# Mamba scan: five of 32 products with B move to ScalarE with time on the partitions, and GpSimd's share is dealt anew

## The reference, cut to what matters

```python
x_in = rn @ in_w.T                         # rn: normalised tokens, 4 x 1024 x 256
x = silu(causal_conv(x_in))                # E = 512 channels
delta = softplus(x @ wd1.T @ wd2.T + wd2_b)
A = -exp(A_log)                            # 512 x 16
Bm, Cm = x @ wB.T, x @ wC.T                # N = 16 values per token each
def step(h, inp):                          # over time
    h = exp(d_l[:, :, None] * A) * h + (d_l * x_l)[:, :, None] * b_l[:, None, :]
    y_l = einsum('ben,bn->be', h, c_l)
```

## Time and profile before

| | us |
|---|---|
| median of 3 runs | 1860.4 (1860.34 to 1862.27) |
| the profiled execution, own time | 1861.13 |
| its span, first to last instruction | 1859.4 |
| VectorE busy over the span | 1471.9 (79%) |
| GpSimd busy | 1100.7 (59%) |
| ScalarE busy | 1074.5 (58%) |
| TensorE matmuls busy | 1708.3 (92%) |

### The profile page before, as it was taken

How to read it: one execution, slowest core, us unless ns; L and a number is a source line. 1 busy time by engine, 2 the same in 40 slices (tenths; PEclk the granted TensorE clock), 3 DMA queues, 4 the chain that set the end, 5 groups by cost and what they waited for, 6 DMA issues and landing times. The chain is left out here.

```text
span 1859.4 us, 26380 instructions
## 1 busy us (share of the span) xinstructions
PE 1708.3 (92%) x9245; PEld 1343.9 (72%) x9245; DVE 1471.9 (79%) x2310; ACT 1074.5 (58%) x1871; POOL 1100.7 (59%) x711
## 2 busy tenths in 40 slices
PE   6888989899898989966889999999999899999999
PEld 2455566565666666655778888888888788888888
DVE  4889999999999999999787767776345586666664
ACT  5877787778778787777534444443443444444442
POOL 2889999999999999999842222220454332222220
PEclk9898999999999999978999999999999999999999
DMA  6223333233333233244011111121000011111111
GB/s 200 81 79 99 107 93 102 87 112 90 108 93 102 94 104 100 95 148 144 7 35 35 35 35 35 35 57 24 7 0 0 1 46 43 46 38 46 46 46 46
DMA packets 113918, 125.63 MB, mean 68 GB/s; under 512 B 18816, under 2 KB 66048, under 8 KB 113664
## 3 DMA queue, kind: packets, MB, share of 16 engines
q1 hardware_dynamic: 113792, 124.03, 22.9%
HBM read 95.14 MB, written 4.72 MB: 54 GB/s over the span
## 5 line engine op out<-in xcount | busy, mean ns | idle before, releaser
L383 POOL TENSOR_TENSOR m_U<-m_U,m_C 128x1024 f32<-128x1024 f32 x255 | 600.6, 2367 | 26.2 <-DVE m_U L890 15.9
L525 PEld LDWEIGHTS m_y<-ident,m_U 128*128 128x128 f32 x2048 | 252.0, 148 | 117.0 <-issue 71.3
L890 DVE TENSOR_TENSOR_SCAN m_U<-m_dA,m_carry,m_U 128x512 f32<-128x512 f32 x256 | 310.8, 1265 | 5.0 <-ACT m_dA L758 4.6
L525 PE MATMUL m_y<-ident,m_U 128*128 128x128 f32 x2048 | 284.4, 285 | 29.2 <-POOL m_U L383 29.0
L890 DVE TENSOR_TENSOR_SCAN m_U<-m_dA,m_U 128x512 f32<-128x512 f32 x256 | 296.2, 1206 | 11.5 <-ACT m_dA L758 8.2
L758 ACT ACTIVATE m_dA<-high,m_negA 128x512 f32<-128x512 f32 x256 | 172.4, 685 | 74.1 <-DVE m_U L890 73.8
L758 ACT ACTIVATE m_dA<-even,m_negA 128x512 f32<-128x512 f32 x256 | 170.8, 684 | 56.1 <-DVE m_U L890 55.1
L1165 POOL TENSOR_TENSOR SW<-g_Rt 128x512 f32<-128x512 f32 x32 | 40.8, 1306 | 253.5 <-DMA g_CT<-SW 235.2
L1165 POOL TENSOR_TENSOR SW<-f_Rt 128x512 f32<-128x512 f32 x32 | 42.0, 1340 | 229.2 <-DMA f_CT<-SW 225.5
L506 PE MATMUL m_psB<-m_stack,m_pick 128*128 128x512 f32 x196 | 101.3, 517 | 33.5 <-DVE m_U L873 33.2
L873 DVE TENSOR_TENSOR m_U<-even,m_psB 128x1024 f32<-128x1024 f32 x100 | 120.0, 1200 | 12.4 <-PE m_psB L506 12.1
(11 more groups left out here) (389 smaller groups left out, 4416.4 us busy)
## 6 DMA issues: line engine op xcount, KB each, us to landing
m_C<-bc_rows SPq DMA_DIRECT2D x256, 256.0 KB, 3.2
m_B<-bc_rows SPq DMA_DIRECT2D x60, 256.0 KB, 3.6
f_CT<-SW SPq DMA_DIRECT2D x128, 64.0 KB, 2.1
g_CT<-SW SPq DMA_DIRECT2D x128, 64.0 KB, 2.0
even<-in_ffn_w SPq DMA_DIRECT2D x16, 256.0 KB, 4.8
f_z_raw<-f_turned_z SPq DMA_DIRECT2D x112, 32.0 KB, 1.9
g_z_raw<-g_turned_z SPq DMA_DIRECT2D x112, 32.0 KB, 1.9
out<-res SPq DMA_DIRECT2D x7, 512.0 KB, 2.8
```

The source lines that it names most:

```text
L383: pool.tensor_tensor(u, u, C[:, M % C_RING, :].unsqueeze(1).to_broadcast([P, PE_E, CHUNK]), ALU.mult).then_inc(hc_ready, 1)
L525: last = nc.tensor.matmul(y[:, t, j * P:(j + 1) * P], U[:, M % U_RING, j, t * P:(t + 1) * P], ident[:, :], start=False, stop=n == N - 1, i ...
L890: nc.vector.tensor_tensor_scan(u, dA[:, s % A_RING, :], u, carry[:, e, n:n + 1] if q else 0.0, ALU.mult, ALU.add).then_inc(scan_done, 1)
```

## The change

Chunk 0 keeps its products as they were. In chunks 1 to 7, units 12 and 14 of the first pass and 2, 4 and 15 of the second (slots 12, 14, 18, 20, 31) are "turned". ScalarE makes their product two units ahead with time on the partitions: B is then one number for each partition, a scale operand, and the product is four activations of 128x256. TensorE turns the result back, four transposes for each half, into the places of the `dA` ring; the decays of such a unit go to an SBUF tile `dAT` instead. The scan reads its decay from `dAT` and its product from PSUM. New jobs turn dx (`tr0` to `tr3`) and B (`bt`) once a chunk. GpSimd's units become (3, 6, 8, 10) and (6, 8, 10, 13) in odd chunks, (3, 6, 9) and (7, 11) in even ones from chunk 2. To make room in SBUF, `C` has three buffers instead of eight and `B` one instead of two; SP issues the fetch of a B row two units earlier than before. Two late jobs (`high0`, `high1`) move to slots 26 and 28, and `FETCH` moves from 8 to 9 units into the last chunk.

```diff
-    U_RING, C_RING, A_RING, B_RING = 6, 8, 3, 2
-    ON_POOL, AHEAD = ((3, 7, 10, 14), (4, 9, 14), (3, 7, 11, 14), (3, 6, 10, 14)), 3
+    U_RING, C_RING, A_RING = 6, 3, 3
+    ON_POOL, AHEAD, B_AHEAD = [((3, 7, 10, 14), (4, 9, 14))] + [((3, 6, 8, 10), (6, 8, 10, 13)), ((3, 6, 9), (7, 11))] * 4, 3, 2
+    TURNED, TURN_AHEAD = [((), ())] + [((12, 14), (2, 4, 15))] * (CHUNKS - 1), 2
...
-                 11: ("cv3",), 12: ("cv3+",), 13: ("out0",), 14: ("out0+",), 15: ("low",), 16: ("low+",),
+                 11: ("cv3",), 12: ("cv3+", "tr2"), 13: ("out0",), 14: ("out0+",), 15: ("tr3", "low"), 16: ("low+",),
...
-                 27: ("out1",), 28: ("out1+",), 29: ("back0",), 30: ("back1",),
+                 27: ("out1",), 28: ("out1+", "tr0"), 29: ("back0",), 30: ("back1",), 31: ("tr1", "bt"),
...
-                if M in pool_units:
-                    i = BEFORE[M]
-                    need(sp, pool_mult, i - B_RING + 1)
-                    sp.dma_start(B[:, i % B_RING, :],
-                                 bc_rows[q, n:n + 1, :].to_broadcast([P, CHUNK])).then_inc(B_ready[i % B_RING], 16)
+                if M + B_AHEAD in pool_units:
+                    n_b = place(M + B_AHEAD)[3]
+                    assert n_b >= B_AHEAD
+                    need(sp, pool_mult, POOL_BEFORE[M + B_AHEAD])
+                    sp.dma_start(B[:, :], bc_rows[q, n_b:n_b + 1, :].to_broadcast([P, CHUNK])).then_inc(B_ready, 16)
...
+            def turn_product(M, j):
+                s = PE_E * M + j
+                pe.wait_ge(UT_ready, TURNED_BEFORE[M] + 1)
+                pe.wait_ge(scan_done, s - A_RING + 1)
+                for t in range(TILES):
+                    last = nc.tensor.transpose(dA[:, s % A_RING, t * P:(t + 1) * P],
+                                               U[:, M % U_RING, j, t * P:(t + 1) * P], ident[:, :])
+                last.then_inc(UT_turned, 1)
...
             for M in range(ALL_UNITS):
-                if M + 2 < ALL_UNITS and M + 2 not in pool_units:
+                if M + 2 in dve_units:
                     spread_B(M + 2)
+                if M + 1 in turned_units:
+                    turn_product(M + 1, 0)
                 for name, k in parts_of(PE_AT, M):
                     part(name, k)
+                if M + 1 in turned_units:
+                    turn_product(M + 1, 1)
...
-                nc.scalar.activation(dA[:, s % A_RING, :], delta[q][:, e, :], ACT.Exp,
+                to = dAT[:, s % PE_E, :] if s // PE_E in turned_units else dA[:, s % A_RING, :]
+                nc.scalar.activation(to, delta[q][:, e, :], ACT.Exp,
                                      scale=negA[:, e, n:n + 1]).then_inc(dA_ready, 1)
+            def product(M):
+                c, q, p, n = place(M)
+                for e in range(PE_E * p, PE_E * (p + 1)):
+                    wait_freed(act, f"tr{e}", c)
+                wait_freed(act, "bt", c)
+                act.wait_ge(nsum_done, M - U_RING + 1)
+                for t in range(TILES):
+                    last = nc.scalar.activation(U[:, M % U_RING, :, t * P:(t + 1) * P], dxT[:, pair(p), t, :], ACT.Copy,
+                                                scale=BT[:, t, n:n + 1])
+                last.then_inc(UT_ready, 1)
...
                     decay(PE_E * (M + 1))
                     decay(PE_E * (M + 1) + 1)
+                if M + TURN_AHEAD in turned_units:
+                    product(M + TURN_AHEAD)
...
+                decay, product = dA[:, s % A_RING, :], u
+                if M in turned_units:
+                    dve.wait_ge(UT_turned, PE_E * TURNED_BEFORE[M] + j + 1)
+                    decay, product = dAT[:, j, :], dA[:, s % A_RING, :]
...
-                nc.vector.tensor_tensor_scan(u, dA[:, s % A_RING, :], u, carry[:, e, n:n + 1] if q else 0.0,
+                nc.vector.tensor_tensor_scan(u, decay, product, carry[:, e, n:n + 1] if q else 0.0,
```

More of the change, by code:

```diff
@@ L129, in mamba @@
         U = sb("U", [P, U_RING, PE_E, CHUNK])
+        pick32 = U[:, 0, 0, 0:2 * N]
         C = sb("C", [P, C_RING, CHUNK])
-        B = sb("B", [P, B_RING, CHUNK])
+        B = sb("B", [P, CHUNK])
+        dxT = sb("dxT", [P, KE, TILES, P])
+        BT = sb("BT", [P, TILES, N])
+        dAT = sb("dAT", [P, PE_E, CHUNK])
         rows = sb("rows", [2 * N, CHUNK])
@@ L151, in mamba @@
         B_full, rows_ready, rows_out = sem("B_full"), sem("rows_ready"), sem("rows_out")
-        B_ready, pool_mult = [sem(f"B_ready{i}") for i in range(B_RING)], sem("pool_mult")
+        B_ready, pool_mult = sem("B_ready"), sem("pool_mult")
+        UT_ready, UT_turned = sem("UT_ready"), sem("UT_turned")
         C_ready = [sem(f"C_ready{i}") for i in range(C_RING)]
@@ L182, in mamba @@
                            (12, "turn0", 9), (12, "turn1", 9), (14, "query", 9), (16, "square", 10), (18, "sum", 11),
-                           (19, "square", 11), (20, "norm", 10), (21, "high0", 0), (22, "turn0", 10),
+                           (19, "square", 11), (20, "norm", 10), (22, "turn0", 10),
                            (22, "turn1", 10), (23, "norm", 11), (24, "query", 10), (25, "turn0", 11),
-                           (25, "turn1", 11), (26, "high1", 0), (27, "query", 11), (29, "back1", CHUNKS - 1)]}
+                           (25, "turn1", 11), (26, "high0", 0), (27, "query", 11), (28, "high1", 0), (29, "back1", CHUNKS - 1)]}
         FIRST_GATE = 10
@@ L191, in mamba @@
         BEHIND = {"out0": -1, "out0+": -1, "out1": -1, "out1+": -1, "gate1": -1, "back2": -1, "back3": -1,
-                  "gate0": 0, "back0": 0, "back1": 0, "silu_g": 0, "sum": 2, "square": 2, "factors": 2, "norm": 2, "double": 2}
+                  "gate0": 0, "tr2": 0, "tr3": 0, "back0": 0, "back1": 0, "silu_g": 0, "sum": 2, "square": 2, "factors": 2, "norm": 2, "double": 2}
         ASKED = dict(enumerate((4, 1, 5, 0), CHUNKS))
@@ L199, in parts_of @@
             late = [(name, k) for slot, name, k in at["late"] if c == CHUNKS - 1 and slot == i]
-            chunks = [(name, k) for name, k in chunks if 0 <= k < CHUNKS and (name, k) != ("back1", CHUNKS - 1)]
+            chunks = [(name, k) for name, k in chunks if 0 <= k < CHUNKS and (name, k) != ("back1", CHUNKS - 1)
+                      and (k > 0 or name[:2] != "tr")]
             return chunks + late
@@ L239, in place, with before @@
             return c, c % 2, i // N, i % N
-        pool_units = [M for M in range(ALL_UNITS) if M % N in ON_POOL[M // N % (2 * PASSES)]]
-        BEFORE = [len([m for m in pool_units if m < M]) for M in range(ALL_UNITS)]
+        pool_units = [M for M in range(ALL_UNITS) if M % N in ON_POOL[M // UNITS][M // N % PASSES]]
+        turned_units = [M for M in range(ALL_UNITS) if M % N in TURNED[M // UNITS][M // N % PASSES]]
+        dve_units = [M for M in range(ALL_UNITS) if M not in pool_units and M not in turned_units]
+        def before(units):
+            return [len([m for m in units if m < M]) for M in range(ALL_UNITS + 1)]
+        POOL_BEFORE, TURNED_BEFORE, DVE_BEFORE = before(pool_units), before(turned_units), before(dve_units)
         def pair(p):
@@ L247, in mamba @@
         SECOND_LAST = UNITS * (CHUNKS - 1)
-        FETCH, PARTS = SECOND_LAST + C_RING, PIECES * KE
+        FETCH, PARTS = SECOND_LAST + 9, PIECES * KE
         block = ctx.enter_context(nc.Block())
@@ L443, in part @@
                     last = mm(take(name, k), [(rnT[:, d, t:t + P], skw[:, d, :]) for d in range(KD)])
+                elif name[:2] == "tr":
+                    e = int(name[2])
+                    pe.wait_ge(dx_ready, KE * k + e + 1)
+                    out = take(name, k)
+                    for t in range(TILES):
+                        last = nc.tensor.transpose(out[:, t * P:(t + 1) * P], dx[q][:, e, t * P:(t + 1) * P],
+                                                   ident[:, :])
+                elif name == "bt":
+                    pe.wait_ge(rows_ready, k + 1)
+                    out = take(name, k)
+                    for t in range(TILES):
+                        last = nc.tensor.transpose(out[:, t * 2 * N:(t + 1) * 2 * N], rows[:, t * P:(t + 1) * P],
+                                                   ident[0:2 * N, 0:2 * N])
                 elif name[:2] == "cv":
@@ L584, in _ @@
             pe.wait_ge(scan_done, PE_E * ALL_UNITS)
[L585 removed]
+            pe.wait_ge(mult_done, len(dve_units))
             pe.wait_ge(gate_done, PASSES * CHUNKS)
@@ L908, in _ @@
             for M in range(ALL_UNITS):
-                if M + 1 < ALL_UNITS and M + 1 not in pool_units:
+                if M + 1 in dve_units:
                     mult(M + 1)
```

33 lines of the change are left out of this document (20 added, 13 removed), and 6 rows, old and new, of the table ACT_AT.

## The result

The changed kernel takes 1873.05 us, median of 6 runs (1869.8 to 1876.3), beside 1862.6 for the kernel before in the same rounds. The ratio is 1.006, 95% interval 1.0046 to 1.0073: slower, by 0.6%. I had forecast 1847 and a range up to 1871. The six executions form two groups, three of 1869.8 to 1871.3 us and three of 1874.8 to 1876.3, and the profiled one is of the second.

What follows compares the result with a forecast made beforehand. VectorE sets the pace, TensorE and GpSimd close behind. Gains of 3.6 us (chunks 1, 3, 5), 6.3 (2, 4, 6) and 4.6 (7), together 14.5, off 1861.1 gave 1846.6, forecast 1847; 8-in-10 range 1829 to 1871.

Steps and rivals of the forecast that it cites:

- The rings and the C landings: C ring of three: landings of 3.3 us, at most 4.1, hidden in 4.7; as a rival 1858 us, chance 0.06.
- the 4 us that I had bounded: Scans of turned units, decay in SBUF and product in PSUM: no change taken, 0.06 us for 70 scans as either end.
- Behind silu_x: Slots 10 to 15: ScalarE's products and a copy delay silu_x, costing VectorE 2.0 us in each of chunks 1 to 6.
- Behind dt0 in odd chunks: Slot 19 behind the gate: unit 20's transposes delay dt0 by 0.44 us and VectorE arrives 1.13 sooner, +1.55 us.
- My own sign of being wrong: One of the listed signs that the forecast is wrong: VectorE's waits over 7 us in odd chunks.
- GpSimd allows at most 33 us: Seven chunks of GpSimd busy time: 710 us against 743.5 now, so a gain of at most 33 us, as much as VectorE's relief.
- I charged 1.0 us of new wait: Chunk 7: 1.0 us in all, for DMA landings of up to 6.9 us at its start beside the FFN weights.
- I took 0.6 us a chunk of new wait: TensorE's added transposes, 100.5 us busy in an odd chunk: 0.6 us of new wait; ends 0 and 4.4.
- VectorE's relief: 29 fewer products on VectorE at 1.13 us: 32.8 us, 5.65 in an odd chunk and 3.4 in an even one.
- I had let 2.0 us of the waits for psB and GpSimd go: Chunks 2, 4, 6: of the waits ending there, 3.9 us in chunk 2, 2.0 go; 2.1 us gained each.
- The rival "ScalarE decides": ScalarE's product takes 2.35 us, on the path four times a chunk, and unit 20's decay comes later: 1872 us, chance 0.14.
- The clock rival: More transposes and fewer spreads lower TensorE's clock in steady chunks to chunk 7's 0.86: 56 us more, 1917 us, chance 0.05.

Runs made afterwards that it cites:

- Four ahead: The changed kernel, but GpSimd makes its product four units ahead instead of three, shares unchanged: 1868.8 us, 1.0043 to the kernel before.
- unit 29 given away: The changed kernel, but VectorE makes unit 29's product in odd chunks, GpSimd seven instead of eight there: 1869.4 us, 1.0042 to the kernel before.
- fewer activations: The changed kernel with one of the four ScalarE activations of each turned product: 1860.65 us, 0.9991 to the kernel before.
- fewer transposes: The changed kernel with one of the four TensorE transposes that turn back each half of a product: 1872.5 us, 1.0053 to the kernel before.
- another order: The changed kernel, but TensorE turns a product's second half ahead of the slot's jobs, not behind them: 1876.0 us, 1.0081 to the kernel before.
- the spaced version: The two repairs together, plus four turned units (8, 12, 18, 31) instead of five in chunks 1 to 6, GpSimd's units re-dealt: 1860.5 us, 0.9992.
- The two repairs together: The changed kernel with chunk 7 dealt as before and GpSimd four units ahead in all chunks: 1862.7 us, 1.0002 to the kernel before.
- the run that changes chunk 7 alone: The changed kernel, but chunk 7 has the old deal, no turned unit and no turning jobs: 1871.1 us, 1.0056 to the kernel before.

## Why the prediction was wrong

**What held.** The product at 1.69 us (1.7 taken). The transposes: eight in 1.04, the last 0.27 included. The rings and the C landings, 3.2 us and at most 4.4 in chunk 3, cost nothing. The turned scan takes 15 ns longer (1273 for 1258 ns with a carry, 1212 for 1197 without), about 1 us in 70 scans, inside the 4 us that I had bounded. Behind silu_x I had 2.3 us of wait in all (2.0 on top of 0.29): measured 1.54, and 0.62 for the turned half of unit 14 ahead of it, 2.2. Behind dt0 in odd chunks 2.7: measured 1.69, and 0.88 for psB ahead of it, 2.6. That these sums agree is in part luck: I had put all of it down to ScalarE's late decay, and a third of it is TensorE's. My own sign of being wrong, waits of VectorE over 7 us in odd chunks, came with 8.6.

**The step that failed first: GpSimd.** "GpSimd allows at most 33 us" treated it as a sum of busy time, 101.8 in an odd chunk. A sum does not say when a product is there. The product of unit M is issued three units ahead, behind the C product of unit M-3. From the end of the scans of M-3 to the start of those of M VectorE takes 6.9 us where it makes two products of its own between. Less GpSimd's product, 2.4, and the C product of M-3, 2.3, this leaves the C products about 2.2 us to lag behind the scans. That time is the same in both kernels (467.5 to 474.4 for unit 30 before, 466.1 to 473.1 for unit 29 after); what grew is the lag. From unit 22 on, two units cost GpSimd 8.2 us (456.62 to 464.82: two C products, a product and a dx job) and VectorE only 5.9 (451.70 to 457.55), since every second product is GpSimd's. So GpSimd lagged 4.6 us at unit 26, ahead of its product for unit 29. In the kernel before it lagged 1.4 us at unit 27, ahead of its product for unit 30. This cost 3.6 us of wait in each of chunks 1, 3 and 5, and no term and no rival held it. Four ahead, and unit 29 given away, both show it: the chunk fell by 2.9 and by 1.2 us.

**Chunk 7.** I charged 1.0 us of new wait and it was 10.3 (14.3 against 4.0). I looked for DMA there, the one thing that proved harmless. With no turned unit and the old deal all of the loss is gone; fewer activations gave 3.3 us back, fewer transposes 0.4, another order made it 0.9 longer. What of the turned units and their deal costs it stays open. TensorE's late jobs wait in order for ScalarE's norm jobs, 4.1 us before and 8.6 after, and spreads and turns queue behind them. It is not ScalarE's product that makes these norms late: with three quarters of it gone the wait is 8.9 us, and the longest, 4.3 us at unit 8, comes before the first product of ScalarE in this chunk. ScalarE's norm job waits there 1.3 us for factors that GpSimd makes behind its product for unit 8, which is VectorE's unit in the old deal. No run has the new deal and no turned unit in chunk 7, or the reverse, so the two are not separated. Nor is the clock, 0.83 to 0.86: the spaced version had chunk 7 2.6 us longer at a lower clock and an equal deal.

**TensorE.** I took 0.6 us a chunk of new wait for its load. The experiment that removed three quarters of the turning saved 0.5 us in chunk 3 and 0.4 in chunk 7, so the size was about right; in the even chunks, with a lower clock, it cannot be told. The waits for TensorE in chunk 3 rose by more, from 0.5 to 1.8 us, and 1.5 of these are the two counted above at silu_x and dt0.

**VectorE's relief.** By busy time it was 4.75 us in chunk 3, not 5.65, and 2.8 in chunks 2 and 4, not 3.4. Two things take most of the rest, as an estimate: ten turned scans at 15 ns, and for each new wait the 0.08 us by which two instructions in a row overlap (two scans 2.45 us, singly 1.265 each).

**The even chunks.** The waits were 5.4 us in chunk 4 against 3.0 before. I had let 2.0 us of the waits for psB and GpSimd go. In chunk 4 they fell only from 2.3 to 2.1, in chunk 2 from 3.9 to 2.2. The gain was 0.3 to 1.9 us against 2.1.

**The sum again, with what was measured.** Odd chunks 1, 3, 5: +9.7 us against -3.6; even: -3.1 against -6.3; chunk 7: +6.5 against -4.6. That is +13.1 against -14.5. Of the +9.7, 1.7 are the wait in slot 17 of chunk 1. Chunk 0 gave 1.3 back, as it did with the small rings and no turned unit at all. The rival "ScalarE decides" had the right sign and 1872, but for another reason: its product never came near 2.35 us. The clock rival did not come in the steady chunks, but for that one wait in chunk 1.

The two repairs together bring the time back to that of the kernel before, and no further. The late product and chunk 7 are therefore enough to account for the change being slower. A product of ScalarE that is nearly free did as much, so these losses are not sums that stand apart from each other. With both repairs chunks 1 to 6 still take 638.0 us; before they took 637.1, and the forecast had 9.9 less. The smaller relief is some 5 us of that. The waits for psB in the even chunks, of which I had let 2.0 us go, are 2.7 to 3.3 us there.

## What to carry to other kernels

A feeder's lead, counted in units, is a time (here 6.9 us for three units), and the feeder's own jobs use it up: work out for each feeder the lag that it has at its densest place, not its sum over the stage. When the bounding engine passes that place faster, the lag grows. A load moved to an engine with idle time costs most where that engine's long jobs (here the function switch, with 0.3 us of wait behind it already) have no slack. Two turned units well ahead of that place, with GpSimd four ahead and chunk 7 as before, gained 0.24%; five spread by slot load, with GpSimd three ahead, lost 0.6%. How much of the difference is the places alone was not measured.

## What the runs showed of the hardware

More transposes did not lower TensorE's clock in the steady chunks. With five turned units, chunks 2, 4, 5 and 6 were granted 1.00; with a quarter of these transposes chunks 1 to 6 had 0.95 to 0.98, and with none, in the kernel before, chunks 2 to 4 had 0.95 to 0.98. The version with no turned unit and four ahead had 1.00 in chunk 3, though, so the transposes are not shown to be what raised it. Part of such differences comes and goes between executions: chunks 1 and 3 had 0.97 and 0.98 in the changed kernel, and 0.99 and 0.97 in the run that changes chunk 7 alone. Chunk 7, where TensorE is idle for 29 to 36 us, had 0.83 to 0.87 in all versions.

An activation of 128x256 from SBUF to SBUF with a pointer scale takes 494 ns, though source and destination are two separate runs of 128 columns each, four in 1.69 us. The exponential of 128x512 takes 711 ns where it is written to SBUF and 683 where it goes to PSUM: 28 ns more for each turned half, which I had not counted. The Trainium skill ("ScalarE: Activation LUTs", section "Step-by-step: what each stage is for") has ScalarE faster to PSUM than to SBUF; the trace agrees, by 4%. A scan with its decay in SBUF and its input in PSUM takes 15 ns longer than the other way round.
